# Where the high and low parts of the expert matmuls stand in SBUF, modulo 512 bytes

## What is computed

```python
x = L0_attn_x                                  # (8, 1024, 256) float32
xn = _layernorm(x, axis=-1)
# s: linear recurrence over time
A = sigmoid(log_A); B_x = xn @ B_w.T + B_b
h_t = A * h_{t-1} + B_x_t;  s = h @ C_w.T + C_b
# g: mixture of 8 experts, the best 2 per token
logits = xn @ Wr + br; top 2, softmax -> c
gate = xn @ W1[e]; up = xn @ W3[e]             # W1, W3: (8, 256, 512)
y = (silu(gate) * up) @ W2[e]                  # W2: (8, 512, 256)
g = silu(sum_e c[e] * y[e])
out = x + s * g
```

## The kernel before

| operand | before | after |
|---|---|---|
| W1, W3 high / low | 0 / 0 | 0 / 64 |
| xh, xl with k = 0 | 192 | 64 |
| xh, xl with k = 1 | 320 | 64 |
| first_xh, first_xl | 0 | 64 |
| hh and hl of even n | 384 and 448 | 448 and 0 |
| hh and hl of odd n | 448 and 0 | 448 and 0 |
| W2 high, low | 0 | 0 |
| odd_W: W1, W3 high / low | 0 / 0 | 0 / 64 |
| odd_xh, odd_xl, odd_hh, odd_hl, odd W2 | 0 | 0 |

## Time and profile before

### The profile page before, as it was taken

One profiled execution on the slowest core, in us unless ns is written; L12 is line 12 of the kernel. 1 busy time (PEld: TensorE's weight loads), 2 busy tenths in 40 slices (PEclk: granted clock), 3 DMA queues, 4 the chain that ended last, 5 costly groups with the idle time before them and its releaser, 6 DMA issues.

```text
span 779.0 us, 17123 instructions
## 1 busy us (share of the span) xinstructions
PE 752.7 (97%) x5381; PEld 675.0 (87%) x5381; DVE 521.8 (67%) x1092; ACT 375.4 (48%) x667; POOL 481.4 (62%) x486
## 2 busy tenths in 40 slices
PE   4999989999999999999999999999999999999897
PEld 2554449999999999999999999999999999998786
DVE  6978976776778667666866665556565765553597
ACT  3985244555455345444554554445455644433440
POOL 4742837788588766846784677468647856563032
PEclk9999999999999999999999999999999999999999
DMA  9999913444555535435544644254446554953897
GB/s 289 336 314 324 159 28 123 123 77 69 132 141 119 108 79 106 75 57 129 139 79 103 158 71 78 44 133 78 93 95 187 104 112 84 309 124 51 260 366 251
DMA packets 101986, 111.15 MB, mean 143 GB/s; under 512 B 15650, under 2 KB 89380, under 8 KB 101892
## 3 DMA queue, kind: packets, MB, share of 16 engines
q0 software_dynamic: 25920, 35.54, 27.4%
q1 hardware_dynamic: 50032, 50.34, 20.4%
q10 hardware_dynamic: 25940, 24.33, 10.4%
HBM read 66.74 MB, written 43.45 MB: 141 GB/s over the span
## 4 chain that ended last, share of the span: by engine, by line
PE 86%; DVE 7%; issue 2%; DMA 2%; ACT 2%; ACTq 0%; DVEq 0%; POOL 0%; POOLq 0%; SPq 0%
PE bank L1582 15%; PE bank L1583 15%; PE bank L1608 15%; PE bank L1584 15%; PE bank L1609 7%; PE bank L1720 6%; PE bank L1482 4%; DVE xnT L1115 2%; PE bank L1570 2%; DVE stats L986 1%; PE bank L1445 1%; PE bank L1635 1%; PE bank L1634 1%; PE bank L1633 1%; DVE xnT L1127 1%
## 5 line engine op out<-in xcount | busy, mean ns | idle before, releaser
L626 POOL DMA_INDIRECT y_rows<-y_sb,token_at x128 | 219.8, 1717 | 130.2 <-DVE y_sb L1233 61.5
L1582 PE MATMUL bank<-parts,W_sb 128*128 128x256 f32 x1008 | 282.9, 281 | 0.1
L1583 PE MATMUL bank<-parts,W_sb 128*128 128x256 f32 x1008 | 281.9, 280 | 0.0
L1584 PE MATMUL bank<-parts,W_sb 128*128 128x256 f32 x1008 | 280.9, 279 | 0.0
L1582 PEld LDWEIGHTS bank<-parts,W_sb 128*128 128x128 f32 x1008 | 189.5, 188 | 2.3 <-DVE parts L1181 0.4
L1583 PEld LDWEIGHTS bank<-parts,W_sb 128*128 128x128 f32 x1008 | 189.4, 188 | 0.0
L1584 PEld LDWEIGHTS bank<-parts,W_sb 128*128 128x128 f32 x1008 | 189.0, 188 | 0.0
L1221 DVE TENSOR_TENSOR hbuf<-hbuf,bank 128x512 f32<-128x512 f32 x128 | 87.4, 687 | 147.9 <-PE bank L1584 144.8
L1608 PE MATMUL bank<-W_sb,parts 128*128 128x512 f32 x512 | 184.5, 401 | 1.2 <-DVE y_sb L1233 1.1
L617 POOL DMA_INDIRECT xg<-xn_rows,token_at x128 | 144.6, 1130 | 38.3 <-POOL token_at L613 18.8
L1609 PE MATMUL bank<-W_sb,parts 128*128 128x256 f32 x512 | 142.6, 279 | 0.0
(11 more groups left out here) (260 smaller groups left out, 925.8 us busy)
## 6 DMA issues: line engine op xcount, KB each, us to landing
x_late<-L_attn_x SPq DMA_DIRECT2D x24, 512.0 KB, 9.4
raw<-L_ffn_W ACTq DMA_DIRECT2D x24, 512.0 KB, 3.8
odd_raw<-L_ffn_W ACTq DMA_DIRECT2D x21, 512.0 KB, 5.4
xn_rows<-h_sb SPq DMA_DIRECT2D x16, 512.0 KB, 6.4
y_rows<-xnT SPq DMA_DIRECT2D x4, 2048.0 KB, 15.7
yy<-y_rows SPq DMA_DIRECT2D x16, 512.0 KB, 9.2
out<-x_late SPq DMA_DIRECT2D x11, 512.0 KB, 7.3
x_kept<-L_attn_x SPq DMA_DIRECT2D x4, 512.0 KB, 6.8
```

Source lines behind the costliest of these rows:

```text
L626: return eng.indirect_dma_start(out=y_rows, out_offset=rows, in_=y, in_offset=None, bounds_check=T + TW - 1, oob_is_err=True, compute_op=A ...
L1582: eng.matmul(part, high, x_h, start=k == 0, stop=False)
L1583: eng.matmul(part, low, x_h, start=False, stop=False)
L1584: last = eng.matmul(part, high, x_l, start=False, stop=k == KD - 1)
```

## The change

The places of the parts in SBUF move; the instructions of each engine, their order and their waits stay, but all lines after L50 are further down by two. `W_sb` and `odd_W` get 128 floats more. The low parts of W1 and W3 start 16 floats (64 bytes) later, W2 starts 128 floats (512 bytes) later. `parts` becomes 128 floats shorter; with `X_STEP` = `TW` the two k of an x part follow each other without a gap, so ScalarE's and VectorE's writes of x parts take the form 128x512 where they had 128x2x256, with the same elements. `H_STEP` goes from 1040 to 1024 floats.

```diff
-LO_AT = W2_AT
+LO_PAD, W2_PAD = 16, 128
+LO_AT, W2_SPLIT = W2_AT + LO_PAD, 2 * W2_AT + W2_PAD
+SPLIT_COLS = 2 * W_COLS + W2_PAD
...
-            W_sb = sb("W_sb", [P, 2 * W_COLS], f32r, mid)
+            W_sb = sb("W_sb", [P, SPLIT_COLS], f32r, mid)
...
-            parts = sb("parts", [P, 5360], f32r, mid)
+            parts = sb("parts", [P, 5232], f32r, mid)
...
-            odd_W = sb("odd_W", [P, 2 * W_COLS], f32r, odd)
+            odd_W = sb("odd_W", [P, SPLIT_COLS], f32r, odd)
...
-            odd_weights = sb("odd_weights", [P, 3 * W_COLS], f32, planning)
+            odd_weights = sb("odd_weights", [P, W_COLS + SPLIT_COLS], f32, planning)
...
-        X_STEP, H_STEP = 288, 1040
+        X_STEP, H_STEP = TW, KI * TW
...
-        xh, xl = x_part(32), x_part(672)
-        hh, hl = h_part(1232), h_part(3296)
-        first_xh, first_xl = (odd_W[:, n * KD * TW:(n + 1) * KD * TW].rearrange("p (k n) -> p k n", k=KD) for n in range(2))
+        xh, xl = x_part(0), x_part(KD * TW)
+        hh, hl = h_part(1120), h_part(3184)
+        first_xh, first_xl = (odd_W[:, LO_PAD + n * KD * TW:LO_PAD + (n + 1) * KD * TW].rearrange("p (k n) -> p k n", k=KD) for n in range(2))
...
             if n == 2:
-                return of[:, 2 * at:2 * (at + cols)].rearrange("p (k s d) -> p k s d", k=KI, s=2)[:, :, low, :]
+                return of[:, W2_SPLIT:W2_SPLIT + 2 * cols].rearrange("p (k s d) -> p k s d", k=KI, s=2)[:, :, low, :]
...
-                        at = 2 * (W2_AT + k * D)
+                        at = W2_SPLIT + 2 * k * D
```

## The result

The changed kernel is slower, by 0.4%. In six runs it took 785.18 us in the median, beside 781.86 for the kernel before: a ratio of 1.0036, with a 95% interval of 1.0023 to 1.0049. A second comparison, in later runs of the same two kernels, gave 785.17 us and 1.0042 (1.0026 to 1.0059). The forecast was 771.2 us. The profiled execution took 783.47 us, 2.4 more than before's.

What follows compares the result with a forecast made beforehand. The prediction took the loop to be bound by TensorE's matmuls, one behind the other. Its terms, -10.1 + 1.0 + 1.3 - 1.3 - 0.3 - 0.5 = -9.9 us, took 781.06 to 771.2 us, range 766.5 to 779.0.

Steps and rivals of the forecast that it cites:

- Step 1: Gate and up: 3024 matmuls from 0.1167 to 0.1133 us, -10.1 us, with 1.0 back for 1008 at 0.1143.
- Step 2: Start of a run: first six steps of the 64 gates that start after a down not gained, 1.3 us back.
- Step 3: Downs with even n: from 2.86 to 2.82 us each, 32 times 0.04, 1.3 us less.
- The odd ones stay: Downs with odd n: claimed to keep their 2.82 us, no change priced.
- Step 4: First products, 48 matmuls: 0.3 us less; odd tile's gate and up, 168 matmuls: 0.5 us less.
- Step 5: Writes of x parts, low W parts, GpSimd's work and loads: priced at nothing.
- the slower one: Rival at L1582 to L1584: level placement puts all 3024 matmuls at 0.1200 us, +10.1; 789.9 us in all; chance 0.08.
- The level third costs: Rival in products: loading low W level with xh puts 1008 steps at 0.1200 us, 6.7 us lost; 778.0 us; chance 0.15.

Runs made afterwards that it cites:

- first grid: TensorE alone, rest of the kernel left out: 64 placements of a product and 64 of a down; low W 0 with x 0 took 288.0 ticks, x 192 272.0.
- fine grid: TensorE alone, rest left out: products with x at 0 to 240 by 16 bytes, five low W places, and downs; before's placement took 280.0 ticks.
- x_only: The kernel before with x's parts alone moved to 64 bytes; 784.43 us, ratio 1.0028 to before.
- x112_low64: The changed kernel with x at 112 bytes where it has 64, low W still 64 bytes on; 780.76 us, ratio 0.9975 to the kernel before.
- x192: The kernel before with both k of the x parts at 192 bytes modulo 512, W and h as before; 781.33 us, ratio 0.999.
- history: TensorE alone, rest left out: seven placements, each behind sixteen different products; low W 0, x 192 took 272.0 ticks twelve times, 282.6 four times.

## Why the prediction was wrong

**What bounds the kernel, and that it is not a wait**: right. The difference in the loop is nearly all one of steps between matmuls; gaps differ by 0.5 to 0.9 us between before and after.

**Step 1, gate and up, -9.1 us**: this failed. The price of a product's matmul was taken over from the down with odd n, as "the least that any f32r case here has", because both would have their weights 64 bytes below or level. Measured: 0.1179, not 0.1133; products +2.2 to +2.5 us. By thirds, the low W's step has 0.1199 where 0.1133 was priced, and the two of high W have 0.1172 and 0.1162. The runs show two errors in it. A product has its own table, in which the placement taken (64 and 64) has 282.4 to 283.2 ticks behind all sixteen predecessors; the placement found from the timeline of another shape says nothing about it. And the direction isn't free: in a product, weights 64 below x (low W at 0, x at 64) gave 282.7 twelve times of sixteen, weights 64 above (x at 192) 272 twelve times, while the down with 448 and 0 runs at 816 as the one with 64 and 0 does in the first grid (the fine grid has 847 for the latter). A hint stood in the earlier trace rows: half of its matmuls had x at 320, which is 64 modulo 256, and they were not at 0.1133.

**Step 2, the start of a run, +1.3 us**: it exists and was understated in kind. It is not only that the better pace comes late; what stands ahead also picks which pace comes. That was the missing idea.

**Step 3, even downs, -1.3 us**: the steady pairs did come to 0.340, but the mean down of even n gained 20 ns, from 2.734 to 2.714 us (its first fifteen steps), 0.6 us in all. **"The odd ones stay"** failed: 2.707 became 2.729, 0.7 us more, with no place of theirs changed. Together the downs gained nothing.

**Step 4**: the odd gate and up gained 0.3 us, where 0.5 was priced; the first two products 0.1, where 0.3 was.

**Step 5, nothing for the other engines**: right; their busy times are the same, and the x parts' other form cost nothing that shows.

**The rivals**: the slower one had its place (L1582 to L1584) and its point of decision right: 0.1171 was named and 0.1179 came. Its mechanism, all three at 0.1200, wasn't: two of three are at 0.1172 and 0.1162. *The level third costs* had its price right, 1008 steps at 0.1200, which is the 0.1199 of low W's step. Its 778.0 us failed because the other two thirds were to come to 0.1133 and stayed near before's 0.1177 and 0.1162. It also placed the level case one step earlier, where low W is loaded while high W works. Whether being level is the cause is not shown: in x_only nothing is level and 90 products are at 0.1178, and x112_low64 pays for its low W without a level pair. From rows 5 to 9 alone I gave 0.84 to faster, on a law in one variable drawn from four points of two shapes. That was too much, with the range's upper end at 779.0 and the slower rival out of it.

**The Trainium skill**: SBUF — State Buffer (Who interferes with whom) of the Trainium skill says that TensorE never waits on anyone. The prediction took from it that no address matters, and the grid decides against that: it has 0.1133 and 0.1200 with TensorE alone. Whether TensorE waits for other engines is not tested there, as none was at work. The places of weights and moving operand act together: with x at 192, low W at 0, 64 and 128 has 272.0, 283.6 and 272.0 ticks, with x at 64 it has 282.6, 282.9 and 285.4. The Trainium skill's 109.2 ns (TensorE: Matmul & The Clock Gate, Back-to-back issue gap, an estimate for 256 columns) is not reached as a steady pace by any f32r placement of ours: 113.3 ns is the lowest of all of them.

**What stays open** is why 16 or 32 bytes matter, and what state of TensorE is carried from one run into the next. The tables say which patterns there are, not what makes them. Whether several profiles of x192 would have other shares wasn't tried.

## What to carry to other kernels

Where TensorE runs matmul behind matmul, read its pace as the time from start to start over some 40 of them, and if two places in one kernel have different paces for the same shape, sweep the operands' start bytes modulo 256 in a small kernel that issues the real order, whole steps with transposes and all. Take a placement that reaches the low pace behind every predecessor that was tried (here x 112 bytes from W, with eight places of h), not one that has it in one row; and don't carry a placement from one order of operands to another.

## What the runs showed of the hardware

- The start addresses of the weights and of the moving operand change the step of an f32r matmul of 256 columns between 0.1133 and 0.1200 us at the same granted clock, with every other engine idle (grid). Most cells 256 bytes apart are the same, and steps of 16 bytes count (x at 96, 112 and 128: 287.9, 272.0 and 284.6 ticks in grid_fine).
- In a given placement the matmuls settle into a pattern, most often of 272, 280, 283 or 288 ticks in the mean. Several placements have two, and which one comes depends on the matmuls ahead (history). In x192 and x_only a product that had settled kept its pattern to its end.
- The lowest was 272 ticks for 256 columns and 816 for a pair of down with 768, each one in sixteen above the number of columns.
- A stretch of 3.4 us at a granted clock of 0.5 (1.2 GHz) in the tail made it 1.7 us longer (x_only). TensorE had waited 2.11 us for VectorE shortly ahead of it; the changed kernel waited 2.00 us at the same place, and its clock stayed full over the stretch behind it.
